# Layer 3 attention in a four-layer kernel: the order of its quads, and the order of the steps on each engine

## The reference, cut to what matters

```
def srel_skew(x):
    b, h, n, _ = x.shape
    v = jnp.pad(x, ((0, 0), (0, 0), (0, 0), (1, 0)))
    return v.reshape(b, h, n + 1, n)[:, :, :n, :]
...
srel = srel_skew(jnp.einsum('bhnd,hmd->bhnm', qx, ex))
qk = (jnp.einsum('bhnd,bhmd->bhnm', qx, kx) + srel) * inv_dim
mask = 1000000000.0 * jnp.triu(jnp.ones((n, n), dtype=x.dtype), 1)
atten = jax.nn.softmax(qk - mask, axis=-1)
out = jnp.einsum('bhnm,bhmd->bhnd', atten, vx).transpose(0, 2, 1, 3).reshape(b, n, d)
return out @ Wp.T + bp
```

## Time and the profile before

| | us |
|---|---|
| median of 3 executions | 3405.09 |
| lowest, highest | 3401.25, 3412.91 |
| profiled execution, its own time | 3411.51 |
| profiled execution, span from first to last instruction | 3409.5 |
| in it, the attention of layer 3 from first to last bias-and-minimum and its drain | 971.3 |

### The profile page before, as it was taken

How to read it: one execution, slowest core, us unless ns; L and a number is a source line. 1 busy time by engine, 2 the same in 40 slices (tenths; PEclk the granted TensorE clock), 3 DMA queues, 4 the chain that set the end, 5 groups by cost and what they waited for, 6 DMA issues and landing times.

```text
span 3409.5 us, 39747 instructions
## 1 busy us (share of the span) xinstructions
PE 2455.0 (72%) x13729; PEld 1328.0 (39%) x13729; DVE 2557.3 (75%) x5554; ACT 1631.6 (48%) x3182; POOL 520.9 (15%) x530
## 2 busy tenths in 40 slices
PE   3697967868678686796823079964777777877778
PEld 1333333333334333343302023323555555555554
DVE  3496999989999999898894757862656666666663
ACT  1345345353453533534323146653666666666652
POOL 0000303003021030210302000031222121221210
PEclk9698978979779787796765579976999999999999
DMA  2001101101101010110100041026777677777741
GB/s 69 2 24 36 38 30 27 32 22 33 35 26 34 22 31 26 30 34 19 37 11 26 23 118 38 1 87 169 214 207 214 202 216 207 201 210 219 205 146 50
DMA packets 312995, 286.88 MB, mean 84 GB/s; under 512 B 16504, under 2 KB 286474, under 8 KB 311226
## 3 DMA queue, kind: packets, MB, share of 16 engines
q1 hardware_dynamic: 312794, 284.34, 29.1%
HBM read 151.45 MB, written 124.45 MB: 81 GB/s over the span
## 4 chain that ended last, share of the span: by engine, by line
DVE 40%; PE 28%; ACT 14%; issue 13%; POOL 2%; DMA 2%; SPq 1%; DVEq 0%; POOLq 0%; ACTq 0%
DVE t L2617 4%; PE banks L2640 3%; PE banks L2684 3%; ACT t L2552 2%; DVE t L1017 2%; PE banks L2601 2%; DVE t L1169 2%; DVE t L952 2%; ACT L144 1%; POOL t L2584 1%; ACT t L1395 1%; DVE t L807 1%; DVE t L808 1%; DVE t L1704 1%; DVE t L1700 1%
## 5 line engine op out<-in xcount | busy, mean ns | idle before, releaser
L2640 PE MATMUL banks<-ident,t 128*128 128x128 f32 x2304 | 391.0, 290 | 132.5 <-ACT xT L2655 47.8
L2617 DVE CUSTOM_DVE_ANT_0 t<-banks,t 128x896 f32<-128x896 f32 (+7 forms) x512 | 381.4, 752 | 138.2 <-PE banks L2603 76.3
L2628 ACT ACTIVATE t<-t 128x896 f32<-128x896 f32 (+7 forms) x512 | 398.5, 779 | 175.6 <-DVE t L2617 175.1
L2640 PEld LDWEIGHTS banks<-ident,t 128*128 128x128 f32 x2304 | 259.9, 144 | 239.0 <-ACT xT L2655 63.8
L2584 POOL TENSOR_TENSOR t<-t 128x512 f32<-128x512 f32 x96 | 122.3, 1274 | 779.0 <-DMA t<-relative_scratch 697.3
L2601 PE MATMUL banks<-t 128*128 128x512 bf16 (+3 forms) x768 | 216.2, 337 | 10.2 <-DVE t L2617 10.1
L548 POOL TENSOR_TENSOR t<-t 128x512 f32<-128x512 f32 x28 | 48.1, 1718 | 914.0 <-ACT t L520 914.0
L1085 PE MATMUL banks<-t 128*128 128x512 f32 x256 | 143.3, 643 | 42.4 <-DVE t L1165 32.6
L1740 ACT ACTIVATE t<-t 128x16 f32<-128x16 f32 x256 | 82.5, 322 | 183.9 <-DVE t L1704 142.3
L1119 ACT ACTIVATE t<-banks 128x512 f32<-128x512 f32 x128 | 76.5, 597 | 191.3 <-PE banks L1085 191.1
L2669 DVE COPY xT<-banks 128x512 f32<-128x512 f32 (+1 forms) x192 | 123.7, 644 | 42.6 <-PE banks L2640 42.6
(11 more groups left out here) (452 smaller groups left out, 6076.4 us busy)
## 6 DMA issues: line engine op xcount, KB each, us to landing
relative_scratch<-t SPq DMA_DIRECT2D x128, 512.0 KB, 5.2
t<-relative_scratch SPq DMA_DIRECT2D x128, 512.0 KB, 4.4
relative_scratch<-t SPq DMA_DIRECT2D x128, 256.0 KB, 5.5
t<-in_wmoe SPq DMA_DIRECT2D x64, 384.0 KB, 3.0
t<-relative_scratch SPq DMA_DIRECT2D x80, 256.0 KB, 3.0
t<-cut_scratch SPq DMA_DIRECT2D x192, 64.0 KB
t<-t SPq DMA_DIRECT2D x16, 512.0 KB, 4.2
cut_scratch<-t SPq DMA_DIRECT2D x8, 768.0 KB, 3.5
```

The source lines that it names most:

```text
L2617: nc.vector.tensor_tensor_reduce(s.s[z][:, 0:n], ps[:, b0:b0 + 1 + i // 4, :].rearrange("p b n -> p (b n)")[:, 0:n], s.bias[r][:, j, WIDE ...
L2628: nc.scalar.activation(s.s[z][:, 0:n], s.s[z][:, 0:n], ACT.Exp, scale=-1.0, bias=s.least[:, z:z + 1]).then_inc(*a.mark("weights", u))
L2640: nc.tensor.transpose(ps[:, 4 + c % 2, (t - lo) * P:(t - lo + 1) * P], s.s[u % NS][:, t * P:(t + 1) * P], k.ident[:]).then_inc(*e.mark("tu ...
```

## The change

The quads of a set are taken in the order of BLOCK, so that those of many and of few blocks alternate; every place that worked out i from the quad's number now looks it up. The scratch has four slots (RS), the rows are made four quads ahead (AHEAD), and SP issues store(q + 1) before load(q). On TensorE, ScalarE and VectorE the work is split in three generators each: "s" the units' scores, weights (minimum or Exp), "t" the turned chunks, "v" rows, values and output; a table of letters for each engine gives the order. The operations themselves, their shapes and the waits that guard the buffers stay.

```diff
-R, NS, NR, AHEAD = 3, 3, 2, 3
+R, RS, NS, NR, AHEAD = 3, 4, 3, 2, 4
 WIDE = T
-BEGUN = 16
+BEGUN = 4
+BLOCK = (7, 0, 6, 1, 5, 2, 4, 3)
...
 def chunks3(u):
-    i = u // JG % NI
+    i = BLOCK[u // JG % NI]
...
-        act.wait_ge(k.queue(f"rel_out{(quad - NR) % R}"), quad - NR)
+        act.wait_ge(k.queue(f"rel_out{(quad - NR) % RS}"), quad - NR)
...
 def rel_out_sp(k, s, quad):
-    sp, r, (e, a, v, g) = k.nc.sync, quad % R, att3_lines(k)
+    sp, r, (e, a, v, g) = k.nc.sync, quad % RS, att3_lines(k)
     out = k.queue(f"rel_out{r}")
     k.sp.wait_ge(a, "rows", quad)
-    if quad >= R:
-        k.sp.wait_ge(k.queue(f"rel_back{r}"), quad - R)
+    if quad >= RS:
+        k.sp.wait_ge(k.queue(f"rel_back{(quad - RS) % R}"), quad - RS)
...
 def rel_back_sp(k, s, quad):
-    sp, r, i, (e, a, v, g) = k.nc.sync, quad % R, quad % NI, att3_lines(k)
+    sp, r, i, (e, a, v, g) = k.nc.sync, quad % R, BLOCK[quad % NI], att3_lines(k)
...
-    k.sp.wait_ge(k.queue(f"rel_out{r}"), quad)
+    k.sp.wait_ge(k.queue(f"rel_out{quad % RS}"), quad)
...
+TURNS4_PE = (
+    "vtsvssvvvvvvsttsssttssttttstvttsvtsvttsvsstvtsstvttsttvttsvvtstvtssstvtsstvtttvsttvttvsstvtstsstvsttsvttsvttvtsv"
...
+TURNS4_ACT = (
+    "vtsvvvvvvssvtststsstssvttsvsvtstssvtstssvtsvtsvtsvtstsstvstsvstsvtstsvtsstvstsvtsvstvstsstvtsssvttssvtsvtstsstvt"
...
+TURNS4_DVE = (
+    "vtsssstststststssvtvsstsvtvstststssvtvsstststvsvtstsstvvstsststvsvtststvsvsststvsvtststsstvsvstststvsvtstsstsvtv"
...
+def rows_order():
+
+    order = [("made", 0)] + [("rows", quad) for quad in range(AHEAD)]
+    for quad in range(QUADS + 1):
+        if quad % (2 * NI) == BEGUN and quad // (2 * NI) + 1 < PAIRS:
+            order.append(("made", quad // (2 * NI) + 1))
+        if quad + AHEAD < QUADS:
+            order.append(("rows", quad + AHEAD))
+        if quad:
+            order.append(("values", quad - 1))
+    return order
...
+def rows_part_pe(k, s, keep):
+    e, a, v, g = att3_lines(k)
+    free6 = free7 = None
+    for what, n in rows_order():
+        yield
+        if what == "made":
+            values_made_pe(k, s, keep, n, free6)
+            free6 = (k.line("made3_act"), "v", n)
+        elif what == "rows":
+            rel_pe(k, s, n, *(x for x in (free6, free7) if x))
+            free6 = free7 = (a, "rows", n)
+        else:
+            yield from values_pe(k, s, n, free7)
+            free7 = (v, "values", n)
...
 def attention_sp(k, s, keep):
+
     stacking = None
+    yield
+    rel_out_sp(k, s, 0)
     for quad in range(QUADS):
         m, step = divmod(quad, 2 * NI)
         if step == 4 and m + 1 < PAIRS:
             stacking = stack_sp(k, s, keep, m + 1)
-        rel_out_sp(k, s, quad)
+        if quad + 1 < QUADS:
+            yield
+            rel_out_sp(k, s, quad + 1)
         if stacking:
             for _ in range(3):
+                yield
                 next(stacking, None)
+        yield
         rel_back_sp(k, s, quad)
-        yield
...
+def side_by_side4_pe(k, s, keep):
+    in_turn(TURNS4_PE, {"weights": scores_part_pe(k, s), "turned": turned_part_pe(k, s), "rows": rows_part_pe(k, s, keep)}, LETTERS4)
```

More of the change, by code:

```diff
@@ L2464 @@
 for _u in range(UNITS):
-    _n = 1 if _u // JG % NI < 4 else 2
+    _n = 1 if BLOCK[_u // JG % NI] < 4 else 2
     _next = -(-_next // _n) * _n % 4
@@ L2474, in by_dve @@
 def by_dve(u, lo):
-    return lo == 0 and (u // JG % NI >= 4 or u % 2 == 0)
+    return lo == 0 and (BLOCK[u // JG % NI] >= 4 or u % 2 == 0)
 def stack_sp(k, s, keep, m):
@@ L2534, in rel_pe @@
     nc, pe, ps, (e, a, v, g) = k.nc, k.pe, k.ps, att3_lines(k)
-    n, i = divmod(quad, NI)
+    n, i = (quad // NI, BLOCK[quad % NI])
     z = n // 2 % 2
@@ L2609, in weights_dve @@
     quad, j = divmod(u, JG)
-    i, r, z, b0 = quad % NI, quad % R, u % NS, SCORE_BANK[u]
+    i, r, z, b0 = BLOCK[quad % NI], quad % R, u % NS, SCORE_BANK[u]
     n = (i + 1) * P
@@ L2723, in attention_act @@
[L2723 to L2743, removed]
@@ L2746, in attention_dve @@
[L2746 to L2762, removed]
+TURNS4_PE = (
+    "vtsvssvvvvvvsttsssttssttttstvttsvtsvttsvsstvtsstvttsttvttsvvtstvtssstvtsstvtttvsttvttvsstvtstsstvsttsvttsvttvtsv"
+    "tsvttvsttvssssttvttstvttsvtstvtssstvtsstvtttvsttvttssvttsvttssvsstvtttvsttvttvsstvtstssvtstsvtttsvttvtsvtsttvsts"
+    "vtssstvttvttssvttvtsvttsvsstvtsstvttsttvttsvvtstvtssstvtsstvtttvsttvttvsstvtsstvtstssvtttsvttvtsvtsvttvsttvsssst"
+    "tvttstvttsvtstvtssstvtsstvtttvsttvttssvttsvttssvsstvtttvsttvttvsstvtstssvtstsvtttsvttvtsvtsttvstsvtssstvttvttssv"
+    "ttvtsvttsvsstvtsstvttsttvttsvvtstvtssstvtsstvtttvsttvttvsstvtsstvtstssvtttsvttvtsvtsvttvsttvssssttvttstvttsvtstv"
+    "tssstvtsstvtttvsttvttssvttsvttssvsstvtttvsttvttvsstvtstssvtstsvtttsvttvtsvtsttvstsvtssstvttvttssvttvtsvttsvsstvt"
+    "sstvttsttvttsvvtstvtssstvtsstvtttvsttvttvsstvtsstvtstssvtttsvttvtsvtsvttvsttvssssttvttstvttsvtstvtssstvtsstvtttv"
+    "sttvttssvttsvttssvsstvtttvsttvttvsstvtstssvtstsvtttsvttvtsvtsttvstsvtssstvttvttssvttvtsvttsvsstvtsstvttsttvttsvv"
+    "tstvtssstvtsstvtttvsttvttvsstvtsstvtstssvtttsvttvtsvtsvttvsttvssssttvttstvttsvtstvtssstvtsstvtttvsttvttssvttsvtt"
+    "ssvsstvtttvsttvttvsstvtstssvtstsvtttsvttvtsvtsttvstsvtssstvttvttssvttvtsvttsvsstvtsstvttsttvttsvvtstvtssstvtsstv"
+    "tttvsttvttvsstvtsstvtstssvtttsvttvtsvtsvttvsttvssssttvttstvttsvtstvtssstvtsstvtttvsttvttssvttsvttssvsstvtttvsttv"
+    "ttvsstvtstssvtstsvtttsvttvtsvtsttvstsvtssstvttvttssvttvtsvttsvsstvtsstvttsttvttsvvtstvtssstvtsstvtttvsttvttvsstv"
+    "tsstvtstssvtttsvttvtsvtsvttvsttvssssttvttstvttsvtstvtssstvtsstvtttvsttvttssvttsvttssvsstvtttvsttvttvsstvtstsstvs"
+    "ttsvttsvttvtsvtsttvstsvtssstvttvttssvttvtstvtssstvtsstvtttvsttvttssvttsvttssvsstvtttvsttvttvsstvtstsstvsttsvttsv"
+    "ttvtsvtsttvstsvtssstvttvttssvttvtstvtssstvtsstvtttvsttvttssttvsttvssssvttttstvttstvsttsssttvsttvstttvttvtvv"
+)
@@ new lines @@
+LETTERS4 = {"s": "weights", "t": "turned", "v": "rows", "b": "biases", "d": "ways"}
+def rows_order():
[8 more added lines that the diff above has]
+    return order
@@ new lines, in scores_part_pe, with turned_part_pe @@
+def scores_part_pe(k, s):
+    for u in range(UNITS):
+        yield
+        scores_pe(k, s, u)
+def turned_part_pe(k, s):
+    for u in range(UNITS):
+        yield from turn_pe(k, s, u)
+def rows_part_pe(k, s, keep):
[12 more added lines that the diff above has]
+            free7 = (v, "values", n)
@@ new lines, in weights_part_act, with turned_part_act, rows_part_act, weights_part_dve @@
+def weights_part_act(k, s):
+    for u in range(UNITS):
+        yield
+        weights_act(k, s, u)
+def turned_part_act(k, s):
+    for u in range(UNITS):
+        yield from turn_act(k, s, u)
+def rows_part_act(k, s):
+    for what, n in rows_order():
+        yield
+        if what == "made":
+            values_made_act(k, s, n)
+        elif what == "rows":
+            rel_act(k, s, n)
+        else:
+            out_act(k, s, n)
+def weights_part_dve(k, s):
+    for u in range(UNITS):
+        yield
+        weights_dve(k, s, u)
@@ new lines, in turned_part_dve, with rows_part_dve, out_act, out_dve @@
+def turned_part_dve(k, s):
+    for u in range(UNITS):
+        yield from turn_dve(k, s, u)
+def rows_part_dve(k, s, keep):
+    for quad in range(QUADS):
+        yield from out_dve(k, s, keep, quad)
+def out_act(k, s, quad):
+    nc, act, (e, a, v, g) = k.nc, k.act, att3_lines(k)
+    act.wait_ge(e, "values", quad)
+    if quad:
+        act.wait_ge(e, "out", quad - 1)
+    nc.scalar.copy(s.out_T[:], k.ps[:, 7, 0:P]).then_inc(*a.mark("out", quad))
+def out_dve(k, s, keep, quad):
+    nc, dve, (e, a, v, g) = k.nc, k.dve, att3_lines(k)
+    (n, i), got = (quad // NI, BLOCK[quad % NI]), k.ps[:, 7, P:2 * P].rearrange("p (j n) -> p j n", j=JG)
+    yield
+    dve.wait_ge(e, "out", quad)
+    nc.vector.reciprocal(s.inv[:], got[:, :, HD]).then_inc(*v.mark())
+    yield
+    dve.wait_ge(v)
+    to = keep.att[:, n // NG * NI + i, n % NG * JG * HD:(n % NG + 1) * JG * HD]
+    nc.vector.tensor_tensor(to.rearrange("p (j d) -> p j d", j=JG), got[:, :, 0:HD], rep(s.inv[:], 2, HD), ALU.mult).then_inc(
+        *v.mark("values", quad))
@@ L2857, in attention3_buffers @@
     nc, s = k.nc, Bag()
-    s.scratch = nc.dram_tensor("relative_scratch", (R, JG, P, QW), F32, kind="Internal").ap()
+    s.scratch = nc.dram_tensor("relative_scratch", (RS, JG, P, QW), F32, kind="Internal").ap()
     s.rel_d = nc.dram_tensor("rel_scratch", (3, P, REL), BF16, kind="Internal").ap()
@@ L2876, in attention3 @@
 def attention3(k, s, keep):
[L2877 to L2881, removed]
+    side_by_side4_pe(k, s, keep)
+    side_by_side4_act(k, s)
+    side_by_side4_dve(k, s, keep)
+    side_by_side4_pool(k, s, keep)
+    side_by_side4_sp(k, s, keep)
     k.meet()
```

45 lines of the change are left out of this document (39 added, 6 removed).

## The result

The changed kernel takes 3258.89 us, median of 4 executions (3253.1 to 3271.89), against 3403.17 for the kernel before (3399.91 to 3412.91): ratio 0.9573, 95% interval 0.955 to 0.9596, 144 us less. The prediction was 3299, with a range of 3238 to 3370. The profiled execution is the slowest of the four, 3271.89 us with a span of 3270.0; against the span of 3409.5 of before that is 139.5 less.

What follows compares the result with a forecast made beforehand. It took waits between engines as the bound: SP's queue and the fixed order. Sixteen sets of 53.3 us, + 10.4 + 2, gave 865 us against 971.3, 106 less than the median 3405.1: 3299 us, range 3238 to 3370.

Steps and rivals of the forecast that it cites:

- likeliest case: Whole kernel: attention sets of 51.5 to 55.3 us, so 3270 to 3331 us; chance 0.55.
- Fuller than I take it: Attention sets: the tables reach the engine share of other stages, 49.3 us a set, 3235 us in all; chance 0.17.
- SP's turn: SP's queue: most of 517.7 us of waiting for landed stores goes; with alternation worth at most 44 us.
- Tables: Order of work on TensorE, ScalarE and VectorE: sets go from 57.3 to 53.3 us, TensorE 85% busy.
- Parts added up: Attention stage: 16 x 53.3 = 852.8, + 10.4 + 2 = 865 us against 971.3, 106 us less.
- A price taken at nothing: SP's loads behind a store in flight: no cost at 4.4 us of landing, a loss from 6.3 us on.
- last rival: Large quads: the load behind the store becomes the bound, VectorE waiting for GpSimd; 3414 us, the edge of slower; chance 0.10.
- Start and end: Ends of the attention stage: first unit about 4 us later, drain about 2 us less, together +2.
- The first set's excess: First set of the stage: its 10.4 us over the mean of the others, 60.05, was left as it is.

Runs made afterwards that it cites:

- e7: The changed kernel without the 24 small loads of the next queries and keys from the third pair of sets on (output differs): 3218.53 us, ratio 0.9443.
- e8: The changed kernel with the small loads issued two or four to a quad over eight quads instead of six over four: 3217.52 us, ratio 0.9445.
- e6: The changed kernel without its tables: fixed lags, alternating quads, store(q+1) before load(q), four scratch slots, AHEAD = 4: 3430.92 us, ratio 1.0058 to the kernel before.
- e5: The kernel before with four scratch slots, store(q+1) before load(q) and AHEAD = 4; ascending quads, fixed lags: 3397.07 us, ratio 0.997.
- e1: The kernel before with four scratch slots and store(q+1) before load(q); AHEAD = 3, ascending quads, fixed lags: 3456.88 us, ratio 1.0133.
- e2: The kernel before with the alternating order of quads alone; fixed lags, old queue order: 3430.48 us, ratio 1.0058.
- e4: The changed kernel with SP issuing store(q), load(q) again, tables and alternation kept: 3397.17 us, ratio 0.9968 to the kernel before.
- e3: The kernel before with four scratch slots, store(q+1) before load(q) and alternating quads; AHEAD = 3, fixed lags: 3470.44 us, ratio 1.0169.

## Why the prediction was right, and where it was off

The direction and the range held: 144 us less where 106 were forecast. The time lies 11 us below the likeliest case (3270 to 3331), and it lies in the range partly by luck. Where no burst of small loads came between, the sets ran at the pace of the rival "Fuller than I take it", and the small loads, which the sum left out, took 41 us of that back. Without their burst e7 and e8 come to 3218, below the range's 3238. In the profiled executions the stage is 151.2 us shorter, 13.2 more lie ahead of its first unit and 1.5 less behind it. The steps one by one:

*SP's turn.* Right as a wait: 517.7 us went to 8.8, into 297 us of waits for ScalarE's rows, which the prediction did not name, and 67 for VectorE's marks on the bias buffers. Wrong as a price. "The most that these two parts give is the step from the ordinary set to the fast one, 60.05 to 57.3: 2.75 x 16 = 44 us": alone the two together cost 22 us (e6). The queue's part is worth 12 us (e5) and costs 47 if the rows are not made four quads ahead (e1); alternation under fixed lags costs 21 (e2). The reading error is in the earlier trace rows: the 2.1 us of the five-block quad were put down to late data, though its own row showed a granted clock of 0.65; e5 has the data and 0.81, and takes 9.2 us. The view of the earlier trace rows would have given a nearer size, since late data reach VectorE through GpSimd's products, and it waited for these 17.2 us in the whole stage:

```profile
DVE t L2617 <- POOL t L2586: 13.8, 12, 3.0
...
DVE t L2617 <- POOL t L2584: 3.4, 2, 2.1
```

*Tables.* The term was 57.3 to 53.3 us a set, 64 us in all. Measured, the stage went from 998.7 us (e6) to 820.1. Two numbers were mis-sized. TensorE's own work was put at 45.43 us a set and called a floor. Since the tables move work over the bound of the sets, two neighbours have to be taken together: in e8 the rows above give 40.57 + 46.51, or 43.5 a set. The pair holds the 16 matmuls that make the values (0.95 us a set), which the set of 45.43 does not, and misses some records (an estimated 0.6 us a set, see the last section). That leaves 43.2, 5% less for the same work at the same clock of 1.00. That matmuls which follow each other closely overlap in this count would explain it, but that is argued and not shown. And the share was put at 85%, the middle between 79 and 92; over those two sets it is 87.08 of 97.1 us, 90%, and 48.6 us a set: close to the rival "Fuller than I take it" with its 92% and 49.3. That ScalarE, VectorE and DMA lie close behind TensorE was the reason for the lower value, and it did not hold: one of the two sets has the DMA engines at 1.00. In the changed kernel the mean set is 51.3, since the small loads take back 2.6 of it.

*Parts added up.* The sum took the queue's gain and the tables' gain as separate terms. They are not: tables and alternation without the queue's part give 13 us, the queue's part without tables 12 (on ascending quads), all but the tables -22, and everything 144. Under fixed lags taking the queue away uncovers little, 12 us; under the tables the old queue binds every quad: in e4 SP waits 577.9 us for landings, and 952.5 us for 128 quads is 7.4 each, where one turn in the earlier trace rows took 8.5.

*A price taken at nothing.* The load behind a store did land later, 5.2 us for 4.4, below the 6.3 at which it would have cost something: right in the sets without small loads, which take 46.1 us each. The last rival's mechanism came true in the others, by a term that the prediction left out, the six small loads that stand on SP between store and load: a landing of 9.72 us and a stall of 5.1, which over the sets costs the 41 us that e8 gives back. The prediction called itself wrong from 50 us of waiting for GpSimd on; past the start it is 7.6 + 31.8 = 39.4. The Trainium skill's rule that was weighed there ("DMA: Bandwidth & Descriptors", "Queues, rings and completion order": a signal lands after every earlier write of its DMA engine) goes the same way as these rows, but no run separates it from plain sharing of the DMA engines.

*Start and end.* +13.2 us at the first unit in place of +4: 7.0 were there at the stage's first matmul and are most likely scatter, as said above, and 6.2 belong to the start that was costed. The first set's excess is 4.8 over the mean of the others, 51.0, instead of 10.4.

## What to carry to other kernels

Before a step between a slow and a fast stretch is booked as the gain of a change, look at the granted clock of both: part of it may be the clock. Two changes that take away two bounds of one loop can be worth little one by one and much together, so price them as a minimum over bounds and not as a sum. In a queue shared by a steady stream and a burst, spread the burst: here issuing the 24 small loads of every second set over eight quads in place of four was worth 41 us.

## What the runs showed of the hardware

The busy time of TensorE is no constant of the work: for the same instructions it was 806 us of the stage in e3, 764 before, 706 in the changed kernel and 692 in e8, falling with the idle time and with a rising granted clock (over the stage 0.90, 0.96, 0.98 and 1.00 in this order). The 706 and the 692 are a little low: 128 of the 8883 matmuls of the stage, all of them scores of 512 columns, have a weight load in the trace and no record of their own. From the gaps that they leave, this is an estimated 10 us of busy time in either. The queue carried 258 GB/s through a whole set of e8 with the DMA engines at 1.00 and the set took the 51.0 us of e7; in the changed kernel the same bytes in a burst, 230 to 265 GB/s over the set, made a load take 9.7 us.
